# Windowed attention scores: padded pairs of heads against single heads on a quarter of the array

## The reference

```python
q = q * cos * scale + rotate_half(q) * sin * scale     # 16 heads of 64
k = k * cos * inv + rotate_half(k) * sin * inv
# windows of 32 queries; each sees its own 32 keys and the 32 before it
sim = jnp.einsum('bhwie,bhwje->bhwij', bq, bk2) * QK_SCALE   # 32 x 64 per head and window
sim = jnp.where(mask, -jnp.finfo(sim.dtype).max, sim)
attn = jax.nn.softmax(sim, -1)
out = jnp.einsum('bhwij,bhwje->bhwie', attn, bv2)
```

## Time and profile before

| what | value |
|---|---|
| median of 3 runs | 3803.61 us (3802.78 to 3813.33) |
| the profiled execution | 3801.54 us |
| its span, first to last instruction | 3799.7 us |
| instructions | 126632 |
| mean granted share of the TensorE clock | 0.933 |
| PE, PE weight loads | 3233.2 us (85%), 2775.9 us (73%) |
| DVE, ACT, POOL busy | 3009.8 us (79%), 2600.9 us (68%), 2503.0 us (66%) |

### The profile page before, as it was taken

How to read it: one execution, slowest core, us unless ns; L and a number is a source line. 1 busy time by engine, 2 the same in 40 slices (tenths; PEclk the granted TensorE clock), 3 DMA queues, 4 the chain that set the end, 5 groups by cost and what they waited for, 6 DMA issues and landing times.

```text
span 3799.7 us, 126632 instructions
## 1 busy us (share of the span) xinstructions
PE 3233.2 (85%) x52674; PEld 2775.9 (73%) x52674; DVE 3009.8 (79%) x4462; ACT 2600.9 (68%) x3787; POOL 2503.0 (66%) x2289
## 2 busy tenths in 40 slices
PE   3444447999989999989999899999899998999996
PEld 2333236788878888778888788888788887888885
DVE  5766767888888788888788887888887888888883
ACT  2222235777777778778787777787687777788775
POOL 1000007887777778778787777887787787788772
PEclk8666668999999999999999999999999999999997
DMA  1000001111111111111111111111111111111111
GB/s 57 0 0 0 0 0 35 37 55 33 33 34 39 57 35 36 36 35 38 57 36 35 30 41 59 36 35 36 34 38 53 36 36 35 37 37 40 30 35 32
DMA packets 54638, 129.97 MB, mean 34 GB/s; under 512 B 10944, under 2 KB 28864, under 8 KB 53312
## 3 DMA queue, kind: packets, MB, share of 16 engines
q1 hardware_dynamic: 54080, 122.02, 11.0%
HBM read 19.25 MB, written 2.10 MB: 6 GB/s over the span
## 4 chain that ended last, share of the span: by engine, by line
PE 56%; DVE 17%; issue 11%; ACT 11%; POOL 5%; DMA 0%; SPq 0%; POOLq 0%; ACTq 0%; DVEq 0%
PE pair L214 44%; PE pair L217 12%; ACT qT L736 6%; POOL qk L959 3%; DVE ss L860 2%; DVE ts L856 2%; DVE pair L873 1%; DVE den L908 1%; ACT sq L726 1%; DVE qk L852 1%; ACT sq L718 1%; POOL Sx L991 1%; DVE qT L359 1%; DVE mx L877 1%; DVE VA L344 0%
## 5 line engine op out<-in xcount | busy, mean ns | idle before, releaser
L980 POOL TENSOR_TENSOR qk<-qk,ts 128x1024 f32<-128x1024 f32 x384 | 910.9, 2383 | 218.8 <-DVE ts L856 205.0
L959 POOL TENSOR_TENSOR qk<-qk,rn 128x1024 f32<-128x1024 f32 x384 | 734.0, 1932 | 43.6 <-issue 28.8
L852 DVE TENSOR_TENSOR qk<-pair,tab 128x1024 f32<-128x1024 f32 x384 | 468.7, 1221 | 370.3 <-ACT sq L718 368.2
L214 PE MATMUL pair<-wq_h,xs_h 128*128 128x512 f32 x1154 | 515.7, 447 | 36.5 <-issue 18.6
L217 PE MATMUL pair<-small,qk 128*128 128x128 f32 x3192 | 452.4, 285 | 79.0 <-ACT qT L736 40.4
L217 PEld LDWEIGHTS pair<-small,qk 128*128 128x128 f32 x3192 | 360.2, 145 | 168.4 <-issue 96.0
L991 POOL TENSOR_TENSOR Sx<-Sx,rden 128x1024 f32<-128x1024 f32 x192 | 365.7, 1905 | 157.3 <-DVE rden L911 157.3
L856 DVE TENSOR_TENSOR ts<-pair,tab 128x1024 f32<-128x1024 f32 x384 | 466.7, 1215 | 0.0
L214 PE MATMUL pair<-wq_h,xs_l 128*128 128x512 f32 x1152 | 465.0, 404 | 0.0
L860 DVE TENSOR_REDUCE ss<-sq 128x16 f32<-128x1024 f32 x384 | 464.6, 1210 | 0.0
L713 ACT ACTIVATE Sx<-Sx 128x1024 f32<-128x1024 f32 x192 | 203.7, 1061 | 378.0 <-DVE Sx L881 378.0
(11 more groups left out here) (201 smaller groups left out, 7079.4 us busy)
## 6 DMA issues: line engine op xcount, KB each, us to landing
VB<-VA SPq DMA_DIRECT2D x192, 384.0 KB, 3.5
VB<-VA SPq DMA_DIRECT2D x96, 128.0 KB, 3.5
wq_raw<-wqkv SPq DMA_DIRECT2D x6, 1536.0 KB, 8.4
xf<-xT SPq DMA_DIRECT2D x96, 64.0 KB, 1.9
xf<-xT SPq DMA_DIRECT2D x96, 63.8 KB, 2.0
wo_sb<-wo SPq DMA_DIRECT2D x6, 512.0 KB, 3.7
out<-X SPq DMA_DIRECT2D x8, 256.0 KB, 2.3
w_raw<-fw SPq DMA_DIRECT2D x6, 341.0 KB, 8.3
```

The lines of the kernel that those rows point to most:

```text
L214: return T_.matmul(out, lhsT, rhs, start=start, stop=stop, **k)
L852: V_.tensor_tensor(h3(qk[:, now, kind, :], DH), h3(source[:, :], DH), rep(tab[:, 2 * kind, b, :], HEADS, DH), ALU.mult)
L959: G_.tensor_tensor(x, x, bc(rn[:, then, kind * HEADS:(kind + 1) * HEADS], HEADS, DH), ALU.mult).then_inc(S["scaled"], 1)
L980: G_.tensor_tensor(qk[:, now, kind, :], qk[:, now, kind, :], ts[:, kind, :], ALU.add).then_inc(S["added"], 1)
```

## The change

qT has no zeros any more: it is the plain transpose of q, two heads in 128 partitions, and ACT copies it out of PC in one instruction. Each score product is split into two, one for each head, with 64 rows (the head's partitions of qT and kT) and 32 columns (its queries); the four products of a head pair and two windows write to partitions 0, 32, 64 and 96 of PB. The values written to PB and their places are those of before. The memset of qT goes.

```diff
-        qT = sb("qT", [P, PAIRS, 4, 2 * WIN])
+        qT = sb("qT", [P, PAIRS, P])
...
-        lane_stats = flat(qT[:, :, :, :])
+        lane_stats = flat(qT[:, :, :])
...
                             to = a * P + pair * KEYS
-                            last = mm(PB[w * KEYS:(w + 1) * KEYS, to:to + KEYS], qT[:, a, 2 * pair + w, :],
-                                      kT[:, a, key0:key0 + KEYS], False, True, skip_group_check=True)
+                            q0 = (2 * pair + w) * WIN
+                            for odd in range(2):
+                                rows = slice(odd * DH, (odd + 1) * DH)
+                                at = w * KEYS + odd * WIN
+                                last = mm(PB[at:at + WIN, to:to + KEYS], qT[rows, a, q0:q0 + WIN],
+                                          kT[rows, a, key0:key0 + KEYS], False, True, skip_group_check=True)
...
-                for odd in range(2):
-                    rows = slice(odd * DH, (odd + 1) * DH)
-                    last = A_.activation(qT[rows, :, :, odd * WIN:(odd + 1) * WIN],
-                                         PC[rows, :].rearrange("p (a w q) -> p a w q", a=PAIRS, w=4), ACT.Copy)
-                last.then_inc(S["qkT_kept"], 1)
+                A_.activation(qT[:, :, :], h3(PC[:, :], P), ACT.Copy).then_inc(S["qkT_kept"], 1)
...
             V_.memset(kT[:, :, 0:WIN], 0.0)
-            V_.memset(qT[:, :, :, :], 0.0)
```

## The result

| kernel | median | lowest to highest | runs |
|---|---|---|---|
| before | 3803.28 us | 3796.41 to 3815.91 | 8 |
| after | 3842.54 us | 3828.96 to 3851.89 | 8 |

The ratio is 1.0094, with an interval of 1.0069 to 1.0118: some 36 us more by the ratio (the two medians are 39 apart), where 6 less were forecast. The profiled execution after took 3849.32 us (span 3847.5), one of the longer ones; the same kernel run again on another occasion had a ratio of 1.0089.

What follows compares the result with a forecast made beforehand. PE's and the vector engine's loops, nearly equal in length, bound the kernel. -21 (q copy, memset) + 0 (scores) + 15 (instruction stalls) = -6 us, median 3798 us; 8 in 10 between 3773 and 3870 us.

Steps and rivals of the forecast that it cites:

- The two loops: PE and vector engine nearly equal: PE's gain shortens w1/gelu (gate) steps, not w2/layer-norm (statistics) steps, where the maximum is late.
- rival 2: PE alone bounds the kernel, so the removed wait is gained in every step: -37 us, 3767 us; chance 0.04.
- The copy of q: Before k's transposes: one copy for two removes PE's L736 wait; with the memset gone -21 us, ends -2 and -52.
- The ceiling of 50 us: Most that removing PE's 140 waits for the q copies (L736) could gain over the whole run.
- The scores: Score matmuls: 128 pairs on four array places overlap at 14.7 ns a pair, 2.1 us, so no change (0).
- Rival 3: Scores' row halves can't write one bank together: 29.6 ns a pair, 4060 us; without any overlap 4770 us; chance 0.14.
- rival 4: Scores' four column groups go slower, 15.5 to 20 ns a pair: +10 to +65 us, 3808 to 3863; chance 0.11.
- The instructions: PE's instruction queue: 24,576 more instructions, 96 packets, bring stalls in the scores: +15 us, bounds 0 and 47.
- The first and the third term: Sum's parts: -21 us for the removed q copy wait and memset, +15 us for instruction stalls in the scores.
- rival 1: No instruction stalls in the scores, so only the -21 us remains: 3783 us; chance 0.15.
- Rival 5: Scores stall for instructions as often as weighing, +47 us in place of 15: +26 us, 3830 us; chance 0.08.
- the likeliest case: The forecast with its neighbours: scores at the old pace, stalls from a few us to 25; 3786 to 3812 us, chance 0.48.

Runs made afterwards that it cites:

- one_copy: Kernel before with plain qT copied once, the 32 score products left unsplit (heads not kept apart): 3783.88 us, ratio 0.9943.
- even_heads: Kernel after with the odd heads' scores left out, 64 pairs a step on two of four places: 3764.23 us, one execution.
- split_only: Kernel before with score products split by head, keeping padded qT, its memset and both half copies: 3836.14 us, ratio 1.0092.
- both_apart: Kernel after with half the scores moved ahead of the last w1 or w2 part, and 3/8 of weighing ahead of q's transposes: 3850.61 us, ratio 1.0124.

## Why the prediction was wrong

**The two loops: right.** Gate steps shortened (15.52 to 15.17 us) and statistics steps did not (15.59). The maximum there is 0.90 us behind scores, where 0.8 was forecast. No profile shows shorter steps of both kinds: rival 2 is out.

**The copy of q: right.** -21 us forecast, -22 measured by `one_copy`, give or take 8. That they agree to 1 us is partly luck. The ceiling of 50 us was never within reach.

**The scores: right.** 2.1 us forecast, 1.99 measured; all four places overlap. Rival 3 (29.6 or 59 ns a pair) and rival 4 (15.5 to 20 ns) are refuted by 13.9 ns. The rule of the Trainium skill, "TensorEngine Tiling (Array Packing)", section "Restrictions and Gotchas", by which different row tiles can't access one PSUM bank simultaneously, does not bind here: the row halves wrote to one bank at 13.9 ns a pair with all four places in use, and at 27.9 with one row half alone (`even_heads`). No run has two row halves in the same partitions of a bank, so that reading of the rule stays open.

**The instructions: this step failed.** The text put it so: "After, they are as dense as weighing, so the bounds are nothing and the same again, 47 us. I take a third, 15 us". The split alone, whose scores cost PE nothing else, measured +35 (`split_only`). The packets were right, 513 against 509. The mechanism was right too, and the bound held for the place it looked at: 30.4 us of issue in the scores, against 47. (The 47 was itself low. The profile before has four waits at the loop's return, 18.6 us in all, which leaves 51 for weighing.) Four things were wrong or left out.

- A third was too small a share. The grounds, that nothing ahead of the scores waits and that the queue has a start, don't hold.
- The new stops weren't only in the scores. Weighing's own issue grew from 24.9 + 26.3 = 51 to 49.7 + 36.5 = 86 us; it has 49 such waits before and 78 after. A packet's end falls anywhere in a step, wherever the instructions are added. Ahead of the q and k projections, where the loop's return is, there are 7 us more (18.6 to 25.4). So the term was to be bounded over the step, not over the phase that gets denser: 73 + 3 us of issue waits in the one profile, 62 + 1 in the other.
- The first and the third term aren't independent. Where the supply binds, PE reaches the missing instruction sooner and waits for it longer; the gain of the copy holds only in steps with no stop. That is why the split alone is +35 and both parts are +34 to +36. The sum took the full 70 waits for the copy and added the stops to them.
- The clock. Between 640 and 3700 us the granted clock stood at 1.2 GHz for 96 us before, and for 150 and 137 us in the two profiles after. The third window above shows what that costs: PE idle for 18.12 - 17.06 = 1.06 us, a mean granted share of 0.91, and 18.12 us in place of 15.17. The missing 0.09 of 18.12 us are 1.6 us, more than the stop itself. 55 us more at half clock are an estimated 27 us of PE's time; with scores that are 0.09 x 192 = 17 us shorter that gives +10, near the 11.9 us by which PE's busy time grew, though this sum leaves out that a phase with a stop in it is longer. But stops alone don't bring the lower clock: `split_only`, with 117 issue waits and +35 us, stood at 1.2 GHz for 102 us, hardly more than before, and PE's busy time there was 3225.0 us, 8 less than before. So the clock is no part of what the split alone costs. In the kernel after, 22 of the 30 stretches at the lower level begin within 1.5 us of the end of a stop (7 of 16 in `split_only`); that the stops bring them is read from that order only, and no run took the stops away and left all else.

Why weighing stops more often, when its own instructions are those of before, is not shown. One possible account is that the supply no longer catches up between the two dense phases of a step. Spreading them out fits (`both_apart` has 20.6 and 19.8 us of issue in the two groups of weighing in place of 36.5 and 49.7), but it changes too much else to prove it.

**The Trainium skill's other rule**, "Runtime: NRT & Kernel Launch", section "Instruction fetch mechanics" (the fetch is hidden by the time to issue each instruction), would have made the sum -21 us, which is rival 1. The 114 stops that all lie at one place of each 256 instructions, and end 1.2 to 1.6 us behind the landing of a packet, speak against it.

**The rivals and the range.** Rival 5 came nearest, with stops in the scores as often as in weighing, +26 us and 3830; what happened is that and more, +36. It had 0.08, and its condition was written as one for the scores alone. The time lies in the range of 3773 to 3870 us, but outside the likeliest case's own 3786 to 3812.

## What to carry to other kernels

Count the instructions that a change adds to the fullest queue, over the whole step, beside the nanoseconds of each: splitting a product in two was free in the array here (1.99 us for 2.08) and still cost 35 us, because the stream was near the rate at which it is supplied. A wait that is removed is worth something only in those steps where neither another engine nor the supply of instructions ends last, so such gains and such losses are not to be added. And look first for the edit that removes the wait and leaves the stream alone: a copy cut in three, with the next work started behind the second, gave -32 us where the rearrangement lost 36.

## What the runs showed of the hardware

- Fp32 products of 64 rows on four places of the array go at 56 ns a place, 13.9 ns a pair with all four in use and 27.9 with two. Two row halves that write one bank, in different partitions, go as fast as in an order that alternates two banks (1.99 and 2.02 us for 128 pairs).
- The instruction queue brings 256 PE instructions of 64 bytes in a packet (8.40 MB in 513), and where PE takes 256 in 2 us it stands still now and then, mostly for 0.4 to 1.8 us, always at the border of two packets, until 1.2 to 1.6 us after the next one has landed. More instructions in one phase bring stops in another.
- A phase that is cut in two takes some 0.2 us longer: 64 split scores 1.10 us, where 128 in one piece take 1.99; a phase that mixes two forms took 2.18 us where either form takes 2.08 or 1.99.
